# A fused attention and FFN block: two sums of the last pair but one through ScalarE and GpSimd, and the attention's additions issued one a body

## The reference, cut to what matters

```python
x = L0_attn_x                                  # (4, 4096, 512) float32
xn = layernorm(x)
x = x + attention(xn, ...) + ffn(xn, ...)

# ffn: every token by itself
s = xn @ Win + bin_                            # 512 -> 64
h = relu(s[..., None] * W1 + b1)               # 64 x 16
g = (h * W2).sum(-1) + b2                      # 64
out = g @ Wout + bout                          # 64 -> 512
# attention: three rounds of an attention among heads and the
# reference's rows; its result is not zero for 16 rows of each batch alone
```

## Time and profile before

| | us |
|---|---|
| median of 3 runs | 326.08 (326.05 to 326.09) |
| the profiled execution | 326.88 |
| its span, from first to last instruction | 325.1 |
| TensorE busy | 295.0 (91%) |
| VectorE busy | 256.8 (79%) |
| GpSimd busy | 237.1 (73%) |
| ScalarE busy | 234.1 (72%) |
| data moved | 87.80 MB, mean 270 GB/s |

### The profile page before, as it was taken

The page is one execution under the profiler, slowest core; times in us unless marked ns, Lnnn a source line. Parts: engine busy times, 40 slices in busy tenths (PEclk is TensorE's granted clock), DMA queues, the critical chain, the costliest instruction groups (busy, mean ns, idle before and its releaser), DMA issues.

```text
span 325.1 us, 5160 instructions
## 1 busy us (share of the span) xinstructions
PE 295.0 (91%) x1804; PEld 131.8 (41%) x1804; DVE 256.8 (79%) x400; ACT 234.1 (72%) x308; POOL 237.1 (73%) x209
## 2 busy tenths in 40 slices
PE   3878499989989999999999989999999999998892
PEld 2644364544433554344443434343434343432220
DVE  0929866589599787897879999999898979995445
ACT  1536655675896869889698668888878788888840
POOL 8434991871992989649892875969879695989950
PEclk9999789999999999999999999999999999999999
DMA  7999949985529999698988999899999999333597
GB/s 232 307 372 404 264 95 326 417 144 194 183 93 334 233 306 320 178 353 240 331 215 293 325 282 328 233 356 279 317 334 344 336 335 316 131 130 151 202 287 282
DMA packets 50569, 87.80 MB, mean 270 GB/s; under 512 B 6360, under 2 KB 35184, under 8 KB 46448
## 3 DMA queue, kind: packets, MB, share of 16 engines
q1 hardware_dynamic: 46400, 65.96, 65.8%
q10 hardware_dynamic: 3504, 21.37, 18.4%
q0 software_dynamic: 640, 0.16, 0.8%
HBM read 53.77 MB, written 33.69 MB: 269 GB/s over the span
## 4 chain that ended last, share of the span: by engine, by line
PE 49%; DVE 28%; DMA 10%; issue 6%; POOL 2%; SPq 2%; ACT 1%; ACTq 0%; DVEq 0%; POOLq 0%
PE op L568 10%; PE s L490 10%; PE g L536 8%; DVE stats L1010 7%; DVE x L983 7%; PE TA L466 6%; DMA xq<-in_L_attn_x_dram 4%; DMA x<-in_L_attn_x_dram 3%; DMA out_dram<-x 3%; PE op L348 3%; PE rep L520 3%; DVE SL L1004 2%; DVE xqT L993 2%; DVE s_full L998 1%; POOL x L1126 1%
## 5 line engine op out<-in xcount | busy, mean ns | idle before, releaser
L1126 POOL TENSOR_TENSOR x<-x,bias_row 128x512 f32<-128x512 f32 x128 | 162.7, 1309 | 2.5 <-DVE bias_row L865 2.5
L743 ACT ACTIVATE H<-rep,b1c,w1c 128x1024 f32<-128x1024 f32 x124 | 142.4, 1221 | 16.6 <-PE rep L520 12.2
L983 DVE TENSOR_TENSOR x<-x,op 128x1024 f32<-128x1024 f32 x59 | 71.4, 1209 | 27.0 <-PE op L568 26.9
L1010 DVE BATCH_NORM_STATS2 stats<-x 128x6 f32<-128x512 f32 x128 | 80.7, 677 | 7.7 <-DMA x<-in_L_attn_x_dram 7.6
L568 PE MATMUL op<-wout,G 64*128 64x512 f32 x236 | 65.0, 627 | 3.6 <-DVE x L983 2.7
L1110 POOL TENSOR_TENSOR rstd<-veps,nhalf 128x8 f32<-128x8 f32 x16 | 26.7, 1671 | 52.7 <-DVE veps L1020 52.6
L536 PE MATMUL g<-H,w2s 128*32 128x512 f32 x512 | 63.4, 600 | 0.0
L718 ACT ACTIVATE xT<-TA 128x512 f32<-128x512 f32 x64 | 38.5, 606 | 30.0 <-PE TA L466 26.6
L490 PE MATMUL s<-xT,win 128*64 128x512 f32 x128 | 58.3, 598 | 0.9 <-ACT xqT L718 0.8
L466 PE MATMUL TA<-ident,x 128*128 128x128 f32 x288 | 48.4, 301 | 6.3 <-DMA x<-in_L_attn_x_dram 3.4
L490 PE MATMUL s<-xqT,winq 128*64 128x512 f32 x112 | 51.1, 598 | 0.0
(11 more groups left out here) (174 smaller groups left out, 289.3 us busy)
## 6 DMA issues: line engine op xcount, KB each, us to landing
out_dram<-x SPq DMA_DIRECT2D x30, 1024.0 KB, 6.0
x<-in_L_attn_x_dram ACTq DMA_DIRECT2D x10, 2048.0 KB, 11.8
xq<-in_L_attn_x_dram SPq DMA_DIRECT2D x112, 128.0 KB, 7.9
x<-in_L_attn_x_dram SPq DMA_DIRECT2D x12, 1024.0 KB, 10.5
out_dram<-x SPq DMA_DIRECT2D x4, 512.0 KB, 3.3
x<-in_L_attn_Wq_dram SPq DMA_DIRECT2D x1, 1024.0 KB, 17.6
x<-in_L_attn_Wk_dram SPq DMA_DIRECT2D x1, 1024.0 KB, 19.7
x<-in_L_attn_Wv_dram SPq DMA_DIRECT2D x1, 1024.0 KB, 17.1
```

The source lines that it names most:

```text
L743: act.activation(Hr[half][k % len(Hr[half])][:, :], rep_banks(n, half)[:, :], ACT.Relu, bias=b1c[:, half, k:k + 1], scale=w1c[:, half, k:k ...
L983: dve.tensor_tensor(both, both, sum_banks(n, j)[:, :].rearrange("p (h d) -> p h d", h=2), ALU.add).then_inc(add_done, 1)
L1010: dve.bn_stats(stats[:, j, :], x_sb[m][:, j * D:(j + 1) * D]).then_inc(bn_done, 1)
L1126: pool.tensor_tensor(x_sb[m][:, c], x_sb[m][:, c], bias_row[:, :], ALU.add).then_inc(xc_done, 1)
```

## The change

In the tail, two of pair N-2's four sums (j = 2 and 3) leave VectorE. ScalarE copies the product from PSUM to SBUF (`take_out`, into the two halves of the by then unused tile `xT`), and GpSimd adds the copy into `x`. `take_out(2)` stands between ScalarE's last relu and `evacuate_g(LAST)`, `take_out(3)` behind it. On TensorE `project(N-2, 3)` moves behind the last two `sum_h`. The store (N-2, 1) now waits for GpSimd's two sums (`taken_added`). The counts of `add_done` are shifted by two.

On GpSimd the attention's additions move: two each for the batches 0, 1 and 2 are issued one at the end of each body 10 to 15, the two of batch 3 after the last `add_bias`, and behind them stand the two sums.

```diff
+        outs = [xT[:, 2 * i:2 * i + 2, :] for i in range(2)]
...
         def store(n, i):
             m = n % RING
-            if n < N - 1:
+            if n == LAST:
+                for j in (2 * i, 2 * i + 1):
+                    sp.wait_ge(add_done, TILES * n + j - 1)
+                    sp.dma_start(out_v[n, :, :, j * D:(j + 1) * D], by_tile(x_sb[m][:, :], j)).then_inc(st[m][i], 16)
+                return
+            if (n, i) == (N - 2, 1):
+                sp.wait_ge(taken_added, 2)
+            else:
                 sp.wait_ge(add_done, TILES * n + 2 * (i + 1))
-                sp.dma_start(out_part(n, i), by_part(x_sb[m][:, :], i)).then_inc(st[m][i], 16)
...
+            sp.dma_start(out_part(n, i), by_part(x_sb[m][:, :], i)).then_inc(st[m][i], 16)
...
+            elif (n, j) in ((LAST, 0), (LAST, 2)):
+                pe.wait_ge(taken, 1 + j // 2)
...
             sum_h(LAST, 1)
-            project(N - 2, 3)
             sum_h(LAST, 2)
             sum_h(LAST, 3)
+            project(N - 2, 3)
...
+        def take_out(j):
+            act.wait_ge(op_done, TILES * (N - 2) + j + 1)
+            act.activation(outs[j - 2], sum_banks(N - 2, j)[:, :], ACT.Copy).then_inc(taken, 1)
...
                 relu(LAST, r)
+            take_out(2)
             evacuate_g(LAST)
+            take_out(3)
...
-            for n in (N - 2, LAST):
-                for j in range(TILES):
-                    add(n, j)
+            add(N - 2, 0)
+            add(N - 2, 1)
+            for j in range(TILES):
+                add(LAST, j)
...
+                if n >= N - 2 * (B - 1):
+                    accumulate((n - (N - 2 * (B - 1))) // 2, n % 2)
...
+            for f in range(2):
+                accumulate(B - 1, f)
+            for j in (2, 3):
+                pool.wait_ge(xc_done, TPP * LAST)
+                pool.wait_ge(taken, j - 1)
+                both = by_tile(x_sb[(N - 2) % RING][:, :], j)
+                pool.tensor_tensor(both, both, outs[j - 2], ALU.add).then_inc(taken_added, 1)
```

More of the change, by code:

```diff
@@ L160, in residual_block @@
         op_done, xc_done, add_done = sem("op_done"), sem("xc_done"), sem("add_done")
+        taken, taken_added = sem("taken"), sem("taken_added")
         (in_xa, in_lna, in_win, in_winq, in_wo2, in_rows, in_small, in_bq, in_scal, in_ffn) = (
@@ L262, in store @@
             m = n % RING
-            if n < N - 1:
-                sp.wait_ge(add_done, TILES * n + 2 * (i + 1))
-                sp.dma_start(out_part(n, i), by_part(x_sb[m][:, :], i)).then_inc(st[m][i], 16)
[L266 to L269, removed]
+            if n == LAST:
[6 more added lines that the diff above has]
+            else:
+                sp.wait_ge(add_done, TILES * n + 2 * (i + 1))
+            sp.dma_start(out_part(n, i), by_part(x_sb[m][:, :], i)).then_inc(st[m][i], 16)
         def sp_program():
@@ L561, in project @@
                 pe.wait_ge(relu_done, TPP * N)
+            elif (n, j) in ((LAST, 0), (LAST, 2)):
+                pe.wait_ge(taken, 1 + j // 2)
             else:
-                free = TILES * n + j - (1 if (n, j) in ((N - 3, 2), (N - 2, 2), (N - 2, 3), (LAST, 0)) else 2 if n == LAST else 0)
+                free = TILES * n + j - (1 if (n, j) in ((N - 3, 2), (N - 2, 2), (N - 2, 3)) else 4 if n == LAST else 0)
                 if free > 0:
@@ L1126, in add_bias, with accumulate @@
             pool.tensor_tensor(x_sb[m][:, c], x_sb[m][:, c], bias_row[:, :], ALU.add).then_inc(xc_done, 1)
+        def accumulate(b, f):
+            n = b * (N // B)
+            pool.wait_ge(att_made, 1)
+            for h in range(2):
+                pool.wait_ge(st[n % RING][h], 16 * (n // RING + 1))
+            pool.dma_start(out[b, 0:LT, f * D // 2:(f + 1) * D // 2], att[f * RW + b * LT:f * RW + (b + 1) * LT, :],
+                           accum_op=ALU.add).then_inc(acc_done, 16)
         def pool_program():
```

## The result

| | before | after |
|---|---|---|
| median us | 326.06 (326.00 to 326.09) | 349.69 (348.37 to 352.34) |
| profiled execution, its span | 326.88, 325.1 | 348.37, 346.6 |
| ratio | | 1.0738 (95%: 1.0697 to 1.0780) |

The changed kernel is 7.4% slower: 23.6 us by the medians, 21.5 by the two spans. The forecast was 3.1. The direction was right and the size wrong by more than six times, for a reason that the prediction did not have.

A forecast was written before the change was run, and what follows sets the result against it. It took the end to be bound by when the first last store is issued plus the bytes still to go. A later issue (0.45) and the half pair (2.6) gave 326.08 + 3.1 = 329.2 us, range 328.0 to 330.4.

The forecast's parts named there:

- Part 5: Bodies 10 to 15: the six moved transfers' issues are absorbed by GpSimd's waits; 0 us, range 0 to +1.0.
- the prediction's own signs of being wrong: Transfers ending under 1.5 us later, the store leaving well ahead of 318, or body 15's rstd moved over 0.5 us.
- Part 1: TensorE's new order in the tail: g done 1.2 us earlier, LAST's adds 1.05 us earlier.
- Part 2: ScalarE's two copies out of PSUM in the tail: 1.22 us each, hidden, at no cost.
- Part 3: GpSimd's two sums in the tail: 2.5 us each, the second ending at 318.2 us.
- Part 4: SyncE's queue: store (N-2, 1) waits until 318.2, LAST's stores behind it, 3.15 MB to go; tail loses 3.1 us.
- Rival (a): The tail ends with VectorE's last adds, not the stores' bytes: 325.1 us or so; chance 4%.
- rival (c): GpSimd's sums in the tail take only 1.06 us each: 327.7 us, or at best no change; chance 6%.
- Rival (b): The loop is re-timed by GpSimd's shifted work and gains more than the tail loses: 324.2 us at lowest; chance 2%.
- Rival (d): GpSimd's issues cost 1.76 us each, making rstd late in bodies 11 and 15: 330.2 to 331 us; chance 6%.

The follow-up runs named there:

- e2: The kernel before with only the attention's additions moved: one at the end of each of bodies 10 to 15, two behind the last bias addition; ratio 1.0652, 346.48 us.
- e3: As e2, but each moved addition is issued before rstd of its body, where GpSimd waits for VectorE; ratio 1.0014.
- e12: As e2, but one bias addition of each eight, the second behind the transfer, waits for the one before it to be done; ratio 1.0018.
- e11: As e2, but SL's second operand is read from PSUM, leaving out the exact low part of s; ratio 0.9971.
- e6: As e5, but the store (N-2, 1) stands behind LAST's first two stores in SyncE's queue; ratio 1.0040, tail 14.79 us.
- e7: The kernel before with TensorE's new order alone, product (N-2, 3) behind the last two sum_h; ratio 1.0050, tail 13.88 us.
- e5: The whole changed kernel, but the six moved additions stand before rstd of their body; ratio 1.0108, tail 16.20 us.
- e9: The kernel before with a single addition moved, to the end of body 10; one execution, 328.23 us.
- e10: The kernel before with a GpSimd memset of 128 x 16 at the end of bodies 10 to 15, additions left at the end; one execution, 324.23 us.

## Why the prediction was wrong, step by step

**Part 5 is the step that failed.** It priced the six moved transfers by GpSimd's own time: 0.8 us each against 1.28 us of slack and more, "I take 0 for this part, with 0 to +1.0", and named as the worst case a late `rstd`. Its arithmetic was right: an issue takes 0.81 to 0.87 us in the bodies, and GpSimd still waits for `veps` in each, 4.2 us in bodies 11 to 15. `rstd` of body 15 does start 9.6 us later than before (291.13, rows 7), which is one of the prediction's own signs of being wrong:

```profile
300.72 1.66 POOL L1125 TENSOR_TENSOR rstd<-veps,nhalf 128x8 f32<-128x8 f32 x1 [4.22 <-DVE veps L1034]
```

But it is VectorE that is late there, not GpSimd. What the prediction lacked is that the transfer changes how GpSimd's next instructions stand to each other, and that this is felt on another engine. e2 has the whole of it (+6.5%), e3 takes it away by the place, e12 by a gap, e11 by the operand. The size is near what the rows give: SL has 20.6 us more (35.1 - 14.5), TensorE's idling for it is 16.4 us more (17.2 - 0.8), and the last relu is 18.7 us later. Part of the SL time is hidden behind other work, and the spells at the lower clock add some time; I did not split these two.

The trace before did hold a warning. SL took 0.67 us in the first bodies and up to 1.85 later, and each that took over 0.7 us ended 0.55 us after an addition of GpSimd. The prediction never asked why one instruction of one shape should vary so. But the trace before held no run of widely overlapping additions, so it could tell of the hold-up, but not of its size.

**Part 1, right.** `G` is done 1.2 us earlier behind the last relu (2.36 for 3.56), the last add 1.2 earlier (1.05 forecast).

**Part 2, right, a little dear.** The copies take 1.06 and 1.02 us, not 1.22, and cost nothing.

**Part 3, right.** 2.35 us each, within 2.1 to 2.6, 0.15 under the value taken. The estimate of 2.25 us from GPSIMD Engine Reference, section Elementwise (Trainium skill) was nearer than my 2.5, by 0.05.

**Part 4, right.** The tail lost 2.8 us where 3.1 were forecast: the 0.3 are mostly the shorter copies and sums. The store left 6.26 us after the last relu (6.5 forecast). e6 and e7 show the two halves of the argument apart: waiting less (e6) or sums on VectorE (e7) reduces the loss as the bytes say. Rival (a), the end set by the adds, is refuted by each of e5 to e7, and rival (c), cheap sums, by 2.35 us. Rival (b), a faster loop, came out the other way: `rstd` comes every 17.7 us in bodies 11 to 15, where before it was 14.4 to 16.9. Rival (d) had the right sign and at most a tenth of the size, and its mechanism did not happen: the issues in the bodies took 0.81 to 0.87 us and not 1.76, and GpSimd never came late.

What stays open: the timed runs of the changed kernel scatter by 4 us, and their median is 1.3 us over the profiled one. Each SL's wait depends on how far GpSimd's run has come when it starts (e2's tail SL took 8.9 us, that of the changed kernel 8.0), which could be the reason; no trace of the slower executions shows it.

## What to carry to other kernels

When work is put on a queue, price more than its duration: look at which instructions follow it there without a wait, and which instruction of another engine is held up by them. An instruction of one shape whose duration varies in the trace can be such a shared resource showing itself. Place transfers issued by GpSimd directly ahead of a wait of GpSimd, not ahead of a run of work. And at a kernel's end, work out when the first waiting store is issued, plus the bytes behind it, before moving any compute: a store that waits holds every store behind it.

## What the runs showed of the hardware that was not expected

- Behind a transfer issued by GpSimd its 128 x 512 additions start 0.2 to 0.3 us before the one ahead ends, where otherwise it is 0.03 to 0.09. It lasts until the first gap: one wait of GpSimd for its own last result ends it (e12), so does a wait for another engine (e9). A memset of 128 x 16 in the same place does not begin it (e10).
- In that state a VectorE subtraction of 128 x 512 with both inputs in SBUF waited up to 8.9 us (e2), to 0.55 us past the end of GpSimd's run; with one input in PSUM it took 0.67 to 0.69 us throughout (e11). Outside that state it waits for the addition that is under way, 1.85 us at most, but for one of 2.34 us in e6 that is not explained.
- The additions themselves gain nothing by it. They start every 1.23 to 1.24 us in either state, and each takes longer: eight of one body 10.1 us (mean of one 1507 ns) in the changed kernel, 9.9 (1272 ns) in the kernel before, neither with an SL let in among them. In e10, where one is, eight take 10.4.
